# Row maxima of an attention carried into a shift row by DMA, with a tile's queries taken every fourth, in a decoder layer on one core

## The reference

```
qkv = hidden_states @ qkv_w.T + qkv_b
xq, xk, xv = split(qkv)                  # 16 query heads, 4 key and value heads, 64 channels
scores = (xq * per-channel scale) @ xk.T
attn = softmax(scores)                   # over all 1024 keys
out = attn @ xv                          # then @ o_w.T + o_b
```

## Time and profile before

| | us |
|---|---|
| median of 3 runs | 2067.19 |
| lowest and highest | 2066.41, 2070.11 |
| the profiled execution's own time | 2067.07 |
| its span, first to last instruction | 2065.3 |
| TensorE busy | 1855.6 |
| VectorE busy | 1378.7 |
| ScalarE busy | 1135.1 |
| GpSimd busy | 979.1 |

### The profile page before, as it was taken

How to read it: one execution, slowest core, us unless ns; L and a number is a source line. 1 busy time by engine, 2 the same in 40 slices (tenths; PEclk the granted TensorE clock), 3 DMA queues, 4 the chain that set the end, 5 groups by cost and what they waited for, 6 DMA issues and landing times.

```text
span 2065.3 us, 27531 instructions
## 1 busy us (share of the span) xinstructions
PE 1855.6 (90%) x9556; PEld 912.9 (44%) x9556; DVE 1378.7 (67%) x2925; ACT 1135.1 (55%) x1507; POOL 979.1 (47%) x763
## 2 busy tenths in 40 slices
PE   3799999988999799998999988998899989998863
PEld 2444453443644344453554435444364434444342
DVE  4466756667576776756578585766657676677656
ACT  1367755655466554655456554665546654575422
POOL 2065545634554444652645345563465535463621
PEclk7799999999999999998999999999899999999895
DMA  4020000000200000010200000010010000000000
GB/s 150 1 62 1 1 1 1 12 21 1 62 11 1 1 21 1 1 32 0 62 11 1 1 0 21 1 32 0 11 41 1 1 0 21 1 1 1 21 0 10
DMA packets 22875, 32.01 MB, mean 15 GB/s; under 512 B 2577, under 2 KB 16977, under 8 KB 22737
## 3 DMA queue, kind: packets, MB, share of 16 engines
q1 hardware_dynamic: 22736, 30.26, 5.3%
HBM read 13.48 MB, written 4.19 MB: 9 GB/s over the span
## 4 chain that ended last, share of the span: by engine, by line
PE 70%; DVE 18%; issue 5%; ACT 4%; POOL 2%; DMA 0%; SPq 0%; POOLq 0%; DVEq 0%; ACTq 0%
PE attended L955 19%; PE key_scores L935 18%; PE misc L853 7%; PE misc L995 5%; PE max_scores L903 5%; DVE relu L1432 3%; PE misc L1019 3%; PE misc L965 2%; PE misc L921 2%; PE misc L1051 1%; PE misc L1010 1%; PE misc L1040 1%; PE misc L858 1%; DVE prob_sum L1446 1%; DVE buf_b L1328 1%
## 5 line engine op out<-in xcount | busy, mean ns | idle before, releaser
L1189 ACT ACTIVATE probs<-key_scores 128x1024 f32<-128x1024 f32 x512 | 524.5, 1024 | 602.1 <-PE key_scores L935 420.6
L1792 POOL TENSOR_TENSOR prob_sum<-prob_sum,probs 128x512 f32<-128x512 f32 x384 | 538.9, 1403 | 234.0 <-ACT probs L1189 212.8
L955 PE MATMUL attended<-probs,v_all 128*64 128x512 f32 x2048 | 577.1, 637 | 0.1
L1432 DVE CUSTOM_DVE_ANT_0 relu<-max_scores,relu 128x512 f32<-128x512 f32 x512 | 332.3, 686 | 263.7 <-PE max_scores L903 262.6
L935 PE MATMUL key_scores<-q_high,k_chain 64*128 64x512 f32 x2048 | 470.2, 455 | 10.7 <-ACT probs L1189 10.3
L935 PEld LDWEIGHTS key_scores<-q_high,k_chain 64*128 64x128 f32 x2048 | 197.4, 189 | 468.3 <-issue 251.5
L1446 DVE TENSOR_TENSOR prob_sum<-prob_sum,probs 128x512 f32<-128x512 f32 x384 | 375.6, 978 | 19.6 <-ACT probs L1189 8.9
L1173 ACT ACTIVATE relu<-max_scores 128x1024 f32<-128x1024 f32 x256 | 261.5, 1021 | 47.2 <-PE max_scores L903 47.2
L903 PE MATMUL max_scores<-k_max,q_high 64*128 64x512 f32 x1024 | 215.5, 416 | 75.4 <-DVE row_max L1432 73.9
L1788 POOL TENSOR_TENSOR prob_sum<-probs 128x512 f32<-128x512 f32 x64 | 87.8, 1371 | 345.6 <-PE misc L965 286.6
L935 PE MATMUL key_scores<-q_low,k_chain 64*128 64x512 f32 x1024 | 207.8, 402 | 0.0
(11 more groups left out here) (406 smaller groups left out, 2170.5 us busy)
## 6 DMA issues: line engine op xcount, KB each, us to landing
k_chain<-k_chain SPq DMA_DIRECT2D x32, 256.0 KB, 3.8
buf_a<-in_x SPq DMA_DIRECT2D x8, 512.0 KB, 4.9
k_max<-k_max SPq DMA_DIRECT2D x16, 256.0 KB, 3.7
x_in<-in_x SPq DMA_DIRECT2D x7, 512.0 KB, 4.2
out_x<-buf_b SPq DMA_DIRECT2D x7, 512.0 KB, 3.0
heads_out<-in_qkv_wT SPq DMA_DIRECT2D x1, 1536.0 KB, 8.5
wo<-in_o_wT SPq DMA_DIRECT2D x1, 1024.0 KB, 12.7
rows_sb<-in_rows SPq DMA_DIRECT2D x1, 646.0 KB, 10.4
```

Of the source, the lines that this page charges most:

```text
L955: tensor.matmul(attended[head * HD:(head + 1) * HD, :], v_all[:, kt, g * HD:(g + 1) * HD], prob_slot(u, kt, head), start=kt == 0, stop=kt ...
L1189: scalar.activation(probs[(u * KT + kt) % len(probs)][:, :, :], key_scores[:, :, :], ACT.Exp).then_inc(S["exp"])
L1432: vector.tensor_tensor_reduce(out=relu[:, head, :], in0=max_scores[:, head, :], in1=relu[:, head, :], scale=1.0, scalar=-3.4e38, op0=ALU.a ...
L1792: gpsimd.tensor_tensor(prob_sum[1][:, :], prob_sum[1][:, :], probabilities, ALU.add).then_inc(S["prob_sum1"])
```

## The change

Four things are edited.

- `max_T` is gone, with its bank. In the diff below the `max_rows` that is added is SP's, and the one that is removed was ScalarE's. `max_rows` moves from ScalarE to SP: for each of the two heads a DMA copies `row_max[u % 2][:, head, :]` (128 partitions with 4 values, 16 bytes each) to one partition of `shift_row[u % 2]`, 512 values in a row. The value of partition p and tile i lands at column 4p + i.
- So the queries of tile `i` are now the columns i, i+4, i+8, ... of `q_high`: the weight load of `max_pair` reads `i:CH:NT`, 128 values 16 bytes apart, where it read 128 neighbours.
- `row_max` becomes [128, 2, 4] and `shift_row` gets a second buffer. The sign moves to `shift_ones`, which holds -1.0.
- `SHIFT_AHEAD` goes from 2 to 4. In the plan the DMAs stand in step 8u-4, the step of the unit's last max pair, and the step that counts as crowded is that one.

```
-Q_AHEAD, MAX_AHEAD, SHIFT_AHEAD, PV_BEHIND, FINISH_BEHIND = 14, 11, 2, 2, 4
+Q_AHEAD, MAX_AHEAD, SHIFT_AHEAD, PV_BEHIND, FINISH_BEHIND = 14, 11, 4, 2, 4
 def shift(plan, u):
-    plan.put_in_bank("max_T", u)
-    yield LATE
     plan.put("max_rows", u)
+    yield
+            def max_rows(u):
+                sp.wait_ge(*after("row_max", "max_s", u, NT - 1))
+                sp.wait_ge(*after("key_scores", "scores", u - 2, 0))
+                sp.wait_ge(*after("padding", "padding"))
+                for head in range(2):
+                    row = shift_row[u % 2][head * HD:head * HD + 1, :].bitcast(F32)
+                    sync.dma_start(row,
+                                   row_max[u % 2][:, head, :]).then_inc(S["max_row"], 16)
-                    tensor.matmul(max_scores[:, head, :], q_high[u % 3][rows, i * P:(i + 1) * P],
+                    tensor.matmul(max_scores[:, head, :], q_high[u % 3][rows, i:CH:NT],
-            def max_T(u):
...
-                for i in range(NT):
-                    done = tensor.transpose(ps[0:HD + 1, i * P:(i + 1) * P], row_max[u % 2][:, i, :], ident)
-            def max_rows(u):
...
-                scalar.activation(shift_row[0:HD + 1, :], bank("max_T", u)[0:HD + 1, :], ACT.Copy,
-                                  scale=-1.0).then_inc(S["max_row"])
-                dve.wait_ge(*after("max_T", "max_T", u - 2))
+                dve.wait_ge(*after("max_row", "max_rows", u - 2))
```

More of the change, by code:

```diff
@@ L96 @@
 SIGNALS = {
-    "ones": {"ones": 1}, "minus_half": {"minus_half": 1}, "padding": {"padding": 7},
+    "ones": {"ones": 1}, "minus_half": {"minus_half": 1}, "padding": {"padding": 6},
     "x_stats": {"bn_stats": NT, "moments": NT, "var_eps": 1, "rstd": 1}, "x_norm": {"normed": NT},
@@ L106 @@
     "max_d": {"max_d": 2, "relu": 1}, "max_s": {"max_s": 2, "row_max": 2},
[L107 removed]
+    "max_rows": {"max_row": 32},
     "scores": {"key_scores": 2, "exp": 1}, "attend": {"attended": 2}, "raw_out": {"raw_out": 1},
@@ L667, in build @@
         q_low = [sb(f"q_low{i}", [P, CH], F32R) for i in range(3)]
-        shift_row = sb("shift_row", [P, CH], F32R)
+        shift_row = [sb(f"shift_row{i}", [P, CH], F32R) for i in range(2)]
         shift_ones = sb("shift_ones", [P, P], F32R)
-        row_max = [sb(f"row_max{i}", [P, NT, HD + 1]) for i in range(2)]
+        row_max = [sb(f"row_max{i}", [P, 2, NT]) for i in range(2)]
         relu = sb("relu", [P, 2, 512])
@@ L836, in k_swap @@
                                    k_chain[at:at + HD, 0, :, half, cols].bitcast(F32)).then_inc(S["k_swap"], 16)
-            stages = {"load": load, "load_x": load_x, "k_swap": k_swap, "residual": residual, "store": store}
+            def max_rows(u):
[6 more added lines that the diff above has]
+                                   row_max[u % 2][:, head, :]).then_inc(S["max_row"], 16)
+            stages = {"load": load, "load_x": load_x, "k_swap": k_swap, "max_rows": max_rows, "residual": residual, "store": store}
             for stage, *key in plan.entries:
@@ L943, in scores @@
                         rows = slice(head * HD, (head + 1) * HD)
-                        tensor.matmul(key_scores[:, head, :], shift_ones[rows, :], shift_row[rows, :],
+                        tensor.matmul(key_scores[:, head, :], shift_ones[rows, :], shift_row[u % 2][rows, :],
                                       start=False, stop=True, skip_group_check=True).then_inc(S["key_scores"])
```

23 lines of the change are left out of this document (6 added, 17 removed).

## The result

| | before | after |
|---|---|---|
| median of the runs, us | 2068.05 | 2114.85 |
| lowest to highest, us | 2066.41 to 2070.11 | 2114.49 to 2119.49 |
| ratio, 95% interval | | 1.0229 (1.0213 to 1.0244) |
| span of the profiled execution, us | 2065.3 | 2113.2 |

A forecast was written before the change was run, and what follows sets the result against it. The prediction took TensorE as the bound, except in tail stretches paced by VectorE. From 2067.07 us it took 31.0 for transposes, added 6.3 for strided loads and 0 for the rest: 2042 us, range 2028 to 2080.

The follow-up runs named there:

- e12: Changed kernel with the crowded step back at 8u-2 and queries in steps of two, plus one step between each tail gate calculation's two parts; 2044.68 us, ratio 0.9892 to before.
- e10: The changed kernel whole, with the second half of every tail one step later still; 2103.24 us, ratio 1.0184 to before.
- e5: The kernel before, with VectorE's statistics of 14 tail normalisations one step later, directly ahead of the normalisation; 2114.9 us, ratio 1.0229.
- e7: The kernel before, with the second half of every tail two steps later; 2084.91 us, ratio 1.0086.
- e4: The changed kernel with the crowded step back at 8u-2, contiguous weight loads, and each tile's maxima sent separately in 512 DMAs; 2055.92 us, ratio 0.9946 to before.

## What to carry to other kernels

An order table is a cost of its own. When a change makes a planner move stages, list for the engines that pace the stretch (here VectorE) what stands between two results that another engine waits for, before and after, and price that list, not the work added. Here it gives the sign; that it gives the size is shown by no run. A burst is cheap when it is cut by the due work or has the other engine's answer ready at its start: in e12 one yield in two places took 2.2 us off the longest step. And when the gain of a step is read off a chain, take it from a stretch at full load and expect part of it back wherever another engine sets the pace.

## What the runs showed of the hardware

**VectorE's normalisation runs at two speeds.** The same instruction took 400 ns or 1418, after's list of the tile:

```profile
L1319 DVE TENSOR_SCALAR buf_b<-buf_a,moments,rstd x56: 400/1418/1477, 309.1 to 1914.3; 128x256 f32<-128x256 f32 x56
```

Four of them filled the 5.49 us from 682.06 on. In this time GpSimd ran five adds and products of 1.26 to 1.31 us each without a gap:

```profile
682.10 1.28 POOL L1782 TENSOR_TENSOR prob_sum<-prob_sum,probs 128x512 f32<-128x512 f32 x1
683.46 1.26 POOL L1791 TENSOR_TENSOR heads_out<-raw_out,inv_sum 128x512 f32<-128x512 f32 x1
684.80 3.94 POOL L1782 TENSOR_TENSOR prob_sum<-prob_sum,probs 128x512 f32<-128x512 f32 x3
```

Each VectorE instruction took about as long as one of GpSimd's. In e10, where the normalisations stand elsewhere, the mean is 825 ns (after: 1273) and the median 402. The Trainium skill ("SBUF — State Buffer", section "SBUF: two separate sides") says that VectorE and GpSimd share one pair of ports, and that whoever starts first holds it for a whole instruction, if VectorE's instruction is in a mode that uses both ports or has two inputs in SBUF. The 1418 ns against 400 fit that. No run here took GpSimd's work away or shows the mode of this instruction, so it is argued, not shown. It isn't what the order costs either: 36 of the 56 took over 1 us before, 48 in after and only 29 in e5, which lost 46.5 us.

**The granted clock shows in the busy time.** The same 141 matmuls of the first eight steps took 30.09 us at a mean granted clock of 0.80 (before) and 25.52 at 0.95 (e7), and the last 254 were busy for 64.71 us at 0.74 and for 73.79 at 0.67.

**Small DMAs within the chip land in 2.0 us**, whether they carry 128 times 16 bytes (after) or 128 times 4 (e4). That is less than the 2.6 us of the nearest small one in the earlier trace rows. There are 512 of them in e4, and TensorE's list of waits names none.
